# Delta rule lead-in: rows 0 and 1 interleaved, the last group's gates behind them, decay scans of rows 4 to 6 from a PSUM bank

## What is computed

```
q = l2norm(silu(h @ Wq)); k = l2norm(silu(h @ Wk)); v = silu(h @ Wv)        # 8 heads
beta = sigmoid(h @ Wb);   alpha = exp(-exp(A_log) * softplus(h @ Wa + dt_bias))
for t in tokens:  S = S * alpha_t;  S += k_t (v_t - k_t S) beta_t;  o_t = q_t S / sqrt(128)
y = (rms_norm(o) * w * silu(h @ Wg)) @ Wo
```

## Time and profile before

| | us |
|---|---|
| median of 3 runs | 1924.22 (1921.43 to 1925.17) |
| the profiled execution | 1930.55, its span 1928.8 |
| PE, DVE, ACT, POOL busy | 1637.9, 1256.8, 1075.3, 865.0 |
| field layer's last turn ends, lead-in begins (PE) | 1016.7 |
| first row's step begins (PE) | 1114.2 |
| loop's last stage before the last layer | to about 1664 |

### The profile page before, as it was taken

How to read it: one execution, slowest core, us unless ns; L and a number is a source line. 1 busy time by engine, 2 the same in 40 slices (tenths; PEclk the granted TensorE clock), 3 DMA queues, 4 the chain that set the end, 5 groups by cost and what they waited for, 6 DMA issues and landing times. The chain is left out here.

```text
span 1928.8 us, 42957 instructions
## 1 busy us (share of the span) xinstructions
PE 1637.9 (85%) x15415; PEld 1172.2 (61%) x15415; DVE 1256.8 (65%) x3303; ACT 1075.3 (56%) x3164; POOL 865.0 (45%) x1080
## 2 busy tenths in 40 slices
PE   0799828994349975999989889999999999899988
PEld 0345417994239972666557767777777777566633
DVE  7586644554344537787776867777777777467757
ACT  0353303442124432888885567777777777777653
POOL 0235673664646651334332877607062534532223
PEclk9996758996569995999999989999999999999989
DMA  2940013423112225000002322222212132221001
GB/s 68 384 137 23 23 45 101 122 79 107 55 54 73 73 89 170 23 28 22 22 20 84 93 66 57 60 65 65 73 40 73 44 78 59 70 53 35 28 12 44
DMA packets 157666, 135.73 MB, mean 70 GB/s; under 512 B 90021, under 2 KB 130279, under 8 KB 155303
## 3 DMA queue, kind: packets, MB, share of 16 engines
q1 hardware_dynamic: 146950, 113.91, 20.1%
q0 software_dynamic: 9088, 18.70, 3.0%
q10 hardware_dynamic: 1440, 0.66, 0.1%
HBM read 76.65 MB, written 56.54 MB: 69 GB/s over the span
## 5 line engine op out<-in xcount | busy, mean ns | idle before, releaser
L848 POOL DMA_INDIRECT y<-moe_y,moe_aim x156 | 177.7, 1139 | 142.8 <-DVE moe_y L988 62.1
L2870 DVE TENSOR_TENSOR delta_sv<-delta_sv,delta_zp 32x256 f32<-32x256 f32 x384 | 161.3, 420 | 114.2 <-PE delta_zp L2443 106.7
L1810 ACT ACTIVATE field_p<-field_sp,field_nm 128x128 f32<-128x128 f32 x512 | 180.2, 411 | 1.5 <-DVE field_nm L1901 1.0
L2783 POOL TENSOR_TENSOR delta_dd<-delta_dd,delta_prod 128x30 f32<-128x30 f32 (+11 forms) x270 | 160.3, 594 | 21.1
L2781 POOL TENSOR_TENSOR delta_prod<-delta_ll,delta_dd 128x30 f32<-128x30 f32 (+11 forms) x270 | 144.9, 537 | 21.2
L2776 POOL TENSOR_TENSOR delta_dd<-delta_ll,delta_minus 128x1024 f32<-128x1024 f32 (+1 forms) x9 | 23.3, 2584 | 275.1 <-DMA delta_ll<-lanes 275.0
L1810 ACT ACTIVATION_READ_ACCUMULATOR field_p<-field_sp,field_nm 128x1 f32 x512 | 128.3, 251 | 0.0
L2443 PE MATMUL delta_zp<-delta_sv,delta_ct 128*32 128x128 f32 x1536 | 122.5, 280 | 4.6 <-DVE delta_sv L2870 4.3
L2854 DVE SCALAR_TENSOR_TENSOR delta_la<-delta_xp,delta_ck,delta_dc 128x256 f32<-128x256 f32 x256 | 107.6, 476 | 9.0 <-PE delta_xp L2401 7.4
L1911 DVE COPY field_pT<-field_ptp 128x512 f32<-128x512 f32 x128 | 84.0, 672 | 36.9 <-PE field_ptp L1660 36.9
L2443 PEld LDWEIGHTS delta_zp<-delta_sv,delta_ct 128*32 128x32 f32 x1536 | 70.2, 109 | 56.6 <-issue 25.0
(11 more groups left out here) (574 smaller groups left out, 4472.8 us busy)
## 6 DMA issues: line engine op xcount, KB each, us to landing
delta_al<-alpha SPq DMA_DIRECT2D x33, 512.0 KB, 4.5
pairs<-c_none SPq DMA_DIRECT2D x16, 1032.0 KB, 16.3
moe_xg<-pairs SPq DMA_DIRECT2D x78, 129.0 KB
moe_yt<-y SPq DMA_DIRECT2D x16, 512.0 KB, 4.7
w_E<-in_E_dram SPq DMA_DIRECT2D x1, 4624.0 KB, 36.7
w_E<-in_E_dram SPq DMA_DIRECT2D x8, 578.0 KB, 4.0
lanes<-delta_la SPq DMA_DIRECT2D x256, 16.0 KB, 1.5
delta_di<-inverses SPq DMA_DIRECT2D x64, 64.0 KB, 2.3
```

What stands on the lines that cost most here:

```text
L848: nc.gpsimd.indirect_dma_start(results, bass.IndirectOffsetOnAxis(ap=aim[:, t % AR, j:j + 1], axis=0), y[:, t % YS, j, :], None).then_inc( ...
L1810: last = nc.scalar.activation(p[:, slot, h, :], s_ps[i][:, k, :], ACT.Exp, bias=nm[:, slot, h:h + 1], accum_out=zs[:, slot, h:h + 1])
L2783: last = nc.gpsimd.tensor_tensor(dd[lanes, a + 1:, 0:a], dd[lanes, a + 1:, 0:a], pr, ALU.subtract)
L2870: nc.vector.tensor_tensor(sv[rows, two, :], sv[rows, two, :], z_ps[2 * pair // HH][rows, at, :], ALU.subtract).then_inc(s["z_kept"], 1)
```

## The change

In the field layer, `alpha_size(0)` moves from batch 1 to batch 0 of group 7, and the eight copies of `diagonal` from behind the last turn into the four batches of group 6, two in each. In the lead-in, TensorE's order becomes: row 0's projections, the first half of row 1's, row 0's norms and key products, the second half of row 1's projections, the first half of row 2's, row 1's norms and key products, `alpha_beta_last`, the second half of row 2's; from row 2 on it is as before. `spread_group(GROUPS - 1)` and `alpha_turn(0)` are issued ahead of the wait for row 0's first silu. ScalarE's copy of the turned factors comes behind all four silus of row 0. The last group's gates and norm come one row later on every engine: `keep_logits_last` after row 1, `scale_last` and `alpha_size(1)` after row 2, `norm_rows_last` after row 3, `alpha_exp`, `alpha_ln` and `alpha_last` of part 1 after rows 4, 5 and 6 on ScalarE, `alpha_turn(1)` behind row 6's key products. SyncE issues `load_first(0)` ahead of a row's alpha load, and `store_norm` a row earlier in its order. After row 3 VectorE writes the two forms of the unit matrix into the bank `w_ps` (`write_starts`), and rows 4, 5 and 6 take their decays by eight scans of 128 elements that read them there (`decays_from_bank`); rows 0 to 3 and 7 and the loop use `decays` as before.

```diff
--- before.py
+++ after.py
@@ -2002,7 +2002,9 @@
                         for i in range(2, HQ):
                             peaks(n + 1, then, i)
                     keep_turned(n, now, 3)
-                    if final and b == 1:
+                    if isinstance(it, int) and half == 0:
+                        diagonal(ch, range(2 * b, 2 * b + 2))
+                    if final and b == 0:
                         alpha_size(0)
                     if final and b == 2:
                         alpha_one(0)
@@ -2018,7 +2020,6 @@
         ch.turn(0, 0, before + (GROUPS - 2) * LINKS)
         turn_groups(TURNS - 1)
         norm_before(B, 1)
-        diagonal(ch)
         alpha_sum(0)
         scale_alpha(GROUPS - 1)
         norm(GROUPS - 1)
@@ -2114,6 +2115,7 @@
         z_ps = [m.ps(f"zp{i}", [128, HH, T]) for i in range(2)]
         n_ps = m.ps("np", [128, GT])
         w_ps = m.ps("wp", [128, HH, T])
+        starts = [w_ps[:, i, :] for i in range(2)]
         k_rows, k_at, q_cols = n_ps[:, 0:2 * T], n_ps[:, 256:256 + H], n_ps[:, 256 + 12:256 + 20]
 
         k_cols = n_ps[:, 256:256 + 2 * H].rearrange("p (c s) -> p c s", c=2)[:, :, 0:HH]
@@ -2312,13 +2314,12 @@
                     sp.dma_start(dram["xpT"][GROUPS + 1, :, half * T:(half + 1) * T], xo[:, half, :]).then_inc(x_stored[half], 16)
                 for k in range(AHEAD):
                     store_lanes(Row(0, k))
+                    if k == GB // 2 - 1:
+                        load_first(0)
                     if k + 2 <= AHEAD:
                         load_alpha(Row(0, k + 2))
-                    if k == GB // 2 - 1:
-                        load_first(0)
-                    if k == GB // 2:
+                    if k == GB - 1:
                         store_norm()
-                    if k == GB - 1:
                         load_first(1)
                     if k == RING - 3:
                         store_beta(1)
@@ -2365,15 +2366,13 @@
 
                 values_last, spread_group, factors_last, output_last, alpha_beta_last, alpha_turn = field_tensor(pe)
 
-                def project_ahead(p, before={}):
+                def project_ahead(p, some):
 
                     pe.wait_ge(hk_in[p.half], p.two * 16 + 16)
-                    for i in range(4):
+                    for i in some:
                         if p.n * 4 + i > 1:
 
                             pe.wait_ge(s["pre_kept"], p.n * 4 + i - 1)
-                        if i in before:
-                            before[i]()
                         project(z_ps[i % 2][:].rearrange("p (h a) t -> p h (a t)", a=2), p, range(2 * i, 2 * i + 2)).then_inc(s["pre_made"], 1)
 
                 def norms(p, before=True):
@@ -2578,34 +2577,40 @@
                 pe.wait_ge(fs["km_made"], MASKED)
                 pe.wait_ge(fs["vm_made"], SPREAD)
 
-                def spread_and_turn():
-                    spread_group(GROUPS - 1)
-                    alpha_turn(0)
-
-                project_ahead(Row(0, 0), {2: spread_and_turn, 3: factors_last})
+                project_ahead(Row(0, 0), range(2))
+                spread_group(GROUPS - 1)
+                alpha_turn(0)
+                project_ahead(Row(0, 0), range(2, 4))
+                factors_last()
+                project_ahead(Row(0, 1), range(2))
                 pe.wait_ge(fs["y_kept"], GROUPS + 1)
                 for k in range(AHEAD + 1):
                     p = Row(0, k)
                     norms(p, k > 0)
                     if k == 0:
                         output_last()
+                    if 1 < k < AHEAD:
+                        project_ahead(Row(0, k + 1), range(4))
                     if k < AHEAD:
-                        project_ahead(Row(0, k + 1), {2: lambda: norm_columns(p)} if k == 0 else {})
+                        norm_columns(p)
                         if k == 0:
                             pe.wait_ge(fs["peak"], SCORED)
                             pe.wait_ge(fs["al_out"], 1)
-                        else:
-                            norm_columns(p)
                         for i in range(2):
                             if k:
 
                                 pe.wait_ge(s["la_kept"], 2 * k + i - 1)
                             key_products(p, i, k == 0)
                         if k == 0:
+                            project_ahead(Row(0, 1), range(2, 4))
+                            project_ahead(Row(0, 2), range(2))
+                        if k == 1:
                             alpha_beta_last()
-                        if k == 1:
+                            project_ahead(Row(0, 2), range(2, 4))
+                        if k == 2:
                             spread_group(GROUPS)
-                        if k == RING - 3:
+                        if k == RING - 2:
+                            pe.wait_ge(s["ck_made"], RING - 1)
                             alpha_turn(1)
                 pe.wait_ge(fs["al_out"], 2)
                 pe.wait_ge(s["la_kept"], 2 * AHEAD)
@@ -2634,6 +2639,8 @@
                         act.wait_ge(s["pre_made"], p.n * 4 + i + 1)
                         nc.scalar.activation(kq[:, p.half, 2 * i:2 * i + 2, :].rearrange("p h t -> p (h t)"),
                                              z_ps[i % 2][:].rearrange("p h t -> p (h t)"), ACT.Silu).then_inc(s["pre_kept"], 1)
+                    if 4 in before:
+                        before[4]()
                     if p.n < AHEAD:
                         load_keys(Row(0, p.n + 2))
                     act.wait_ge(s["pre_kept"], p.n * 4 + 4)
@@ -2739,12 +2746,12 @@
                 keep_factors_last, keep_sum_last, alpha_exp, alpha_ln, alpha_last = field_scalar(act, load_first_keys)
                 tokens_read(act)
                 for k in range(AHEAD + 1):
-                    keep_ahead(Row(0, k), {2: (keep_factors_last, keep_sum_last)[k]} if k < 2 else {})
-                    if k == 3:
+                    keep_ahead(Row(0, k), ({4: keep_factors_last}, {2: keep_sum_last})[k] if k < 2 else {})
+                    if k == 4:
                         alpha_exp(1)
-                    if k == 4:
+                    if k == 5:
                         alpha_ln(1)
-                    if k == 5:
+                    if k == 6:
                         alpha_last(1)
                 for n in ("be_stored", "al_stored"):
                     act.wait_ge(fs[n], 32)
@@ -2843,6 +2850,17 @@
                     dve.wait_ge(al_in[p.half], p.two * 16 + 16)
                     dcf = dc[:, p.half, :, :].rearrange("p h t -> p (h t)")
                     ch.later(nc.vector.tensor_tensor_scan(dcf, al[:, p.half, :], eye[:].rearrange("p h t -> p (h t)"), 0.0, ALU.mult, ALU.add))
+
+                def write_starts():
+                    dve.wait_ge(fs["h_kept"], GROUPS + 2)
+                    nc.vector.tensor_copy(starts[0].rearrange("p (g t) -> p g t", t=BL), w["ident"][:].rearrange("p (g t) -> p g t", t=BL))
+                    ch.link(nc.vector.tensor_copy(starts[1].rearrange("p (g t) -> p g t", t=BL), turned(w["ident"][:])))
+
+                def decays_from_bank(p):
+                    dve.wait_ge(al_in[p.half], p.two * 16 + 16)
+                    for h in range(H):
+                        last = nc.vector.tensor_tensor_scan(dc[:, p.half, h, :], al[:, p.half, h * T:(h + 1) * T], starts[kind(h)], 0.0, ALU.mult, ALU.add)
+                    ch.later(last)
 
                 def keep_la(p, i, some=range(HH)):
                     if some.start == 0:
@@ -3019,8 +3037,8 @@
                         last = nc.vector.tensor_copy(at_kind(ball_at[lanes_of(part), :, :], 1), of_kind(ball[lanes_of(part ^ CROSS), :, :], 1))
                     ch.link(last)
 
-                def diagonal(links):
-                    for h in range(H):
+                def diagonal(links, heads):
+                    for h in heads:
                         one = turned(w["ident"][:]) if kind(h) else w["ident"][:].rearrange("p (g t) -> p g t", t=BL)
                         last = nc.vector.tensor_copy(eye[:, h, :].rearrange("p (g t) -> p g t", t=BL), one)
                     links.link(last)
@@ -3041,18 +3059,21 @@
                         dve.wait_ge(fs["a_stored"], STEADY)
                         dve.wait_ge(fs["h_stored"], STEADY)
                     keep_rows(p)
-                    decays(p)
+                    if HT <= k < RING - 1:
+                        decays_from_bank(p)
+                    else:
+                        decays(p)
                     keep_columns(p, kn[:, p.slot, :], qe[:, p.slot, :])
                     for i in range(2):
                         keep_la(p, i)
-                    if k == 0:
+                    if k == 1:
                         keep_logits_last()
-                    if k == 1:
+                    if k == 2:
                         scale_last()
                         alpha_size(1)
-                    if k == 2:
+                    if k == 3:
                         norm_rows_last()
```

(2 more changed lines are left out.)

## The result

Over 17 runs of each kernel, side by side, the median went from 1925.17 to 1919.09 us; the ratio of changed to before is 0.9976, with a 95% interval of 0.9967 to 0.9985. The forecast was 12.1 us (0.63%); measured are 4.6 us by the ratio. The sign is right, the size is not, although the 1919.1 us lie inside the given range. The profiled run took 1915.60 us with a span of 1913.8, where that of before took 1930.55: as a pair they flatter the change, since the changed kernel's trace is already 8.3 us ahead at a store that no edit had reached (`hT` of group 5 is issued at 943.02 us, before at 951.30). So I compare stretches between two events of the same trace, never positions in the span.

What follows compares the result with a forecast made beforehand. Holes of TensorE in the field layer's tail and the lead-in were taken as the bound, the loop being full. Terms 4.6 + 6.0 + 1.5 = 12.1 us off the 1924.22 median gave 1912.1 us, range 1906 to 1920.5.

Steps and rivals of the forecast that it cites:

- Part A: Field layer's tail: earlier alpha_size(0) and moved copies, net -4.6 us, bounds -0.7 to -6.4.
- The size's share: Group 7: earlier alpha_size(0) removes 3.6 us of stall and 2.8 us of lower clock, its operations charged 0.9 us.
- +0.9 us for the eight copies in group 6: Group 6: half of the copies' 2.05 us charged, since VectorE has short waits there.
- all of the moved work on the path: Field layer's tail, low bound: moved work costs 2.9 us and the clock stays low, net -0.7 us.
- delaying group 6 in full: Rival: copies do this in group 6 and rows don't gain, cancelling nearly all; chance 0.04.
- Part B: Lead-in to first step: 2.3 us of SyncE's wait for GpSimd plus 3.7 from rows, -6.0 us, bounds -2.3 to -9.5.
- the rows: Lead-in: row 6's keep_la ends 3.7 us earlier; rival that rows don't gain gives 1915.8 us, chance 0.18.
- the bank scans: Lead-in: three free 5.7 us of GpSimd, eight short scans take 2.7 us; they hardly matter for the first step.
- The hole ahead of row 2's norms: Lead-in, TensorE: a new hole of some 2.6 us ahead of these norms.
- charging half of a fall: Lead-in, row 2: the new hole may lower the clock at 3.1 us; 1.5 us charged.
- the interleaving: Lead-in, rows 0 and 1: keep_la of row 1 done 4.5 us earlier, so an earlier inversion, no earlier row 2.
- Part C: Inverses of rows 4 to 7: TensorE's wait shrinks from 2.1 to 0.6 us, -1.5 us, between 0 and -2.1.

Runs made afterwards that it cites:

- experiment 1: The changed kernel with the eight copies back behind the field layer's last turn: 1911.86 against 1923.49 us for the kernel before, ratio 0.9934.
- experiment 2: The kernel before with only the eight copies moved into the four batches of group 6: ratio 1.0037 to the kernel before, 7.2 us slower.
- experiment 5: The changed kernel with three, three, two and no copies in the four batches of group 6: ratio 0.9997 to the kernel before.
- experiment 6: The changed kernel with four, three, one and no copies in the four batches of group 6: ratio 0.9981 to the kernel before.
- experiment 8: The changed kernel with copies behind the last turn and all lead-in decay scans from SBUF, none from the bank: ratio 0.9932 to the kernel before.
- experiment 4: The changed kernel with four copies in each of batches 0 and 1 of group 6, none in batches 2 and 3: ratio 0.9932 to the kernel before.
- experiment 11: The changed kernel with copies between scale_alpha and norm, and SyncE writing the first inverses ahead of row 6's block stores: ratio 0.9929 to the kernel before.
- experiment 3: The kernel before with only alpha_size(0) moved one batch earlier: ratio 0.9969 to the kernel before, 6 us.
- experiment 7: The kernel before with only the lead-in's part of the change, copies and alpha_size(0) as before: ratio 0.9972 to the kernel before.
- experiment 9: The changed kernel with copies behind the last turn and rows 0 and 1 projected one after the other, bank scans kept: ratio 0.9933 to the kernel before.
- experiment 10: The changed kernel with copies behind the last turn, rows 0 and 1 one after the other, all decay scans from SBUF: ratio 0.9942 to the kernel before.

## Why the prediction was half right

**Part A failed, in one term.** The size's share held: -5.6 against -5.5, stall and clock as worked out. The step that failed is the sum's "+0.9 us for the eight copies in group 6", half of their 2.05 us, and with it the bound: "all of the moved work on the path" stopped at 2.05 plus the size's 0.9. The copies cost 6.0 us in group 6, of which the traces give 0.4 to the wait behind batch 0's pair, 1.1 to the delay in batch 2 and 4.6 to TensorE's clock. In group 7 the lower clock comes once more (0.75 from 990 to 995 us, where experiment 1 has 1.00), behind a wait of 1.14 us that both kernels have, and takes some 1.5 us. It belongs to the copies as well: all four kernels whose clock fell in group 6 (the changed one, experiments 2, 5 and 6) ran the `field_yT` wait's matmuls of group 7 at the lower clock (1.81 to 1.94 us), and none of the nine others did (1.08), seven of them behind the same 1.14 us. About as much came back from group 7's `aT` store to the first projection (10.4 us, before 11.8). That is no gain of the change: this stretch takes 9.1 us in experiment 8 and 12.1 in experiment 1, with the copies at the same place, as TensorE holds the full clock in it or doesn't. That the two cancel in this pair of traces is luck. The 2.05 us that I started from weren't the copies' own time either: all eight take 1.24 us in experiment 4, and behind the last turn an operation of GpSimd lies beside them. I had priced the copies by their own duration and VectorE's slack. I had not asked what GpSimd does beside each pair, though my own argument on the scans rested on that very contention, nor let a hole of under 1 us bring the clock down, having charged the clock only behind those of 2.7 and 3.6 us. I did write down the tell ("wrong in A if group 6 gets longer by more than 1 us"), and it is what the trace shows. The rival nearest to it, that something cancels nearly all with the copies "delaying group 6 in full", had the place but not the price.

**Part B held: 6.2 us against 6.0,** though so near a hit is partly luck. In parts: row 6's `keep_la` ends 78.3 us after the first projection, before 83.3, so the rows gave 5.0 where I had 3.7 (in the span it ends 12.8 us earlier, but 8.3 of these were there before any edit was reached); SyncE's 2.3 us wait for GpSimd is down to 0.1, as forecast. Back came 1.0: from the write to TensorE's first step are 8.2 us instead of 7.2. That time runs from 7.2 to 10.3 us over the traces but experiment 11's, in which the write goes ahead of other stores, and issuing the write takes 2.64 us in experiment 3 with the old lead-in and 1.78 in experiments 5 and 6 with the new, so neither is shown to come from the change. The mean of the six traces is 92.6, of the three with the old lead-in 97.6 (97.44, 96.86 and 98.34), which says 5.0 for B; a single trace is good to some 2 us here. What I said of the bank scans also held: no operation of the inversion above 0.7 us beside them (0.59 at 1067.71), 2.59 us for eight against the 2.7 taken, the inversion 39.3 us against 41.1, and by experiment 8 they hardly matter for the first step. The estimate of 3.1 us from the Trainium skill's page "VectorE: DVE Perf Modes" was too high by 0.5. The hole ahead of row 2's norms is 2.63 us (forecast 2.6), with norms at the lower clock behind it (1.94 against 1.07) and the full one by the next row's key products. Experiments 1, 4 and 11 have the same hole of 2.63 us and run these norms in 1.07 us; in experiments 5, 6 and 7 the clock fell as in the changed kernel, in 8 in part (1.30). So charging half of a fall was fair, and which of the two a trace shows is chance as far as these runs tell.

**My account of the interleaving was too generous.** I gave it, with the move of `alpha_beta_last`, 4.5 us of earlier inversion; experiments 9 and 10, which leave that move in, say at most 2.9 and 1.2 for the interleaving alone (36.1 us with it in experiment 1, 38.9 and 37.3 without). The whole is more than the forecast all the same: the inversion starts 7.0 us earlier after the first projection, where I had 5.2, so the other moves did more than I gave them. Bank scans and interleaving each remove the same wait of SyncE, so that with one of them the other is idle, and experiment 10 shows that without both the rows come 3 us sooner and the loss is under what the time resolves.

**Part C failed in its size**: the term was 1.5 us, the wait shrank by 0.3, and the stretch from the first step on grew by 0.2. SyncE sets the chain, as forecast, and its write comes 2.8 us earlier after the first step (31.7 us, before 34.5), but from the write to the last lane load are 7.5 us where they were 5.7. The inverses arrive 0.9 us earlier, and TensorE comes to its wait for them 0.6 us earlier too. Why these transfers land later I haven't tested.

**The loop** didn't change, as forecast. All told, 12.1 less the copies' extra 5.1 (6.0 for 0.9) and the 1.7 that are missing from the first step on, and B's 0.2 on the other side, is the 5.5 of the table: the medians say 6.1, the ratio 4.6. What beats both kernels is experiment 1, or 4: the change with its copies at a place where no wait of TensorE hangs on them or only a short one, 0.66 to 0.68% faster than before.

## What to carry to other kernels

A small operation that is moved beside other work has to be priced against the engine that shares its ports at that very place, not by its duration and its engine's slack: go through the target stretch row by row and look for the neighbour. Where TensorE is nearly full, a new wait on it can have two prices, itself and the clock behind it: here 1.1 us and 4.6, and 1.5 more in the next group. Before crediting a move with a gain, ask what it costs the chain beside the one that it helps: interleaving and bank scans helped GpSimd, and SyncE's chain, which decides, paid. When one edit bundles several, give each its own bound, since here one part ate another's gain and the sum looked like a small success.

## What the runs showed of the hardware that I had not expected

- One 128x128 float copy of VectorE, some 0.2 us alone, took 1.14 us beside a 1.04 us GpSimd operation that began at the same time (by the records the copy began 0.02 us ahead, and it was the one that stood).
- A wait of TensorE of 0.89 us (0.95 with three copies per batch ahead) stood before a fall to the 1.2 GHz level in all four profiled kernels that had it (the changed one, experiments 2, 5 and 6), at 4.6 to 4.8 us each; none of the nine others fell in group 6. It is not the hole alone. Waits of 1.02 us for `field_yT` in group 6 (experiments 4 and 6) left the clock full. And in experiment 4's trace the clock fell at the same place of an earlier group, right behind the small matmuls of L1687, with no wait at all:

```profile
906.08 1.98 PE L1653 MATMUL field_sp<-field_km,field_qT 32*128 32x512 f32 x4
```

- A fall tends to come back. Behind that one (3.0 us lost) the next wait for `field_yT`, 17 us later, came with a second (1.6 us lost), where experiment 1's trace, with no fall ahead, has the same wait at the full clock; experiment 8's trace shows the same pair one group earlier, all in code that no edit touches. Group 7 above is the same again. TensorE of experiment 4, then of experiment 1:

```profile
923.40 1.93 PE L1668 MATMUL field_yp<-field_pT,field_vm 128*32 128x128 f32 x32 [0.57 <-DVE field_yT L1916]
```
```profile
923.46 1.08 PE L1668 MATMUL field_yp<-field_pT,field_vm 128*32 128x128 f32 x32 [0.60 <-DVE field_yT L1916]
```

  Why the first fall comes in some traces and not in others stays open.
- A scan of 128 elements with one input in PSUM runs every 0.32 us (2.59 for eight) and leaves GpSimd alone; one of 1024 over SBUF takes 2.28 us and stopped it for 1.9.
